# Ten VectorE pieces instead of twelve for a log series, with a new loop and end order

## The reference

```
xBC = zxbcdt[..., D_INNER:D_INNER + CONV_DIM]
dt = softplus(zxbcdt[..., -H_M:] + dt_bias)          # 8 heads
xBC = silu(conv_b + causal_conv4(xBC, conv_w))       # xh 512, B 128, C 128
A = -exp(A_log)
h_t = h_{t-1} * exp(dt_t * A) + (dt_t * xh_t) outer B_t
y_t = h_t @ C_t + D_skip * xh_t
out = resid + rms(y * silu(z), gnorm_w) @ out_proj_w
```

## Time and profile before

| what | value |
|---|---|
| median of three runs | 1319.52 us (1319.49 to 1320.14) |
| profiled execution: its span | 1319.5 us |
| granted TensorE clock | 1.00 in every window |
| TensorE matmuls busy | 1303.4 us, 99% |
| VectorE busy | 1193.6 us, 90%, 3032 instructions |
| ScalarE busy | 1131.2 us, 86% |
| GpSimd busy | 947.7 us, 72% |
| chain that ended last | TensorE 92%, VectorE 4%, GpSimd 2% |

### The profile page before, as it was taken

How to read it: one execution, slowest core, us unless ns; L and a number is a source line. 1 busy time by engine, 2 the same in 40 slices (tenths; PEclk the granted TensorE clock), 3 DMA queues, 4 the chain that set the end, 5 groups by cost and what they waited for, 6 DMA issues and landing times.

```text
span 1319.5 us, 43916 instructions
## 1 busy us (share of the span) xinstructions
PE 1303.4 (99%) x15877; PEld 1165.5 (88%) x15877; DVE 1193.6 (90%) x3032; ACT 1131.2 (86%) x3407; POOL 947.7 (72%) x1214
## 2 busy tenths in 40 slices
PE   8999999999999999999999999999999999999998
PEld 7888888999888898888998888899888889898887
DVE  6999999999999999999999999999999999999882
ACT  6778888898888898888898888899888899888866
POOL 4777777777777777777677777687777677677674
PEclk9999999999999999999999999999999999999999
DMA  6121122212122212122211122211122222011210
GB/s 208 48 74 50 50 74 78 78 49 67 50 70 78 78 50 66 50 70 78 78 57 59 50 70 78 78 60 57 50 70 78 77 82 62 17 51 58 66 49 25
DMA packets 41285, 87.03 MB, mean 66 GB/s; under 512 B 5744, under 2 KB 10992, under 8 KB 41072
## 3 DMA queue, kind: packets, MB, share of 16 engines
q1 hardware_dynamic: 40560, 83.93, 20.4%
q10 hardware_dynamic: 512, 0.31, 0.1%
HBM read 75.53 MB, written 8.68 MB: 64 GB/s over the span
## 4 chain that ended last, share of the span: by engine, by line
PE 92%; DVE 4%; POOL 2%; issue 1%; DMA 1%; ACT 1%; DVEq 0%; ACTq 0%; POOLq 0%
PE bank L332 28%; PE bank L442 11%; PE bank L573 7%; PE bank L432 5%; PE bank L399 5%; PE bank L456 5%; PE bank L556 5%; PE bank L587 4%; PE bank L692 4%; PE bank L627 3%; PE bank L380 3%; PE bank L648 3%; PE bank L677 2%; PE bank L490 2%; PE bank L436 1%; PE bank L531 1%
## 5 line engine op out<-in xcount | busy, mean ns | idle before, releaser
L991 DVE SCALAR_TENSOR_TENSOR ACC<-bank,cw,ACC 128x250 f32<-128x250 f32 (+2 forms) x576 | 264.5, 462 | 6.4 <-ACT ACC L1561 3.7
L332 PE MATMUL bank<-xnT,wnl 128*128 128x256 f32 x640 | 198.6, 310 | 1.7 <-DVE XC L1004 1.4
L1648 ACT ACTIVATE PC<-bank,stc 128x128 f32<-128x128 f32 x512 | 182.8, 388 | 8.0 <-DVE stc L1103 5.2
L332 PE MATMUL bank<-xnL,wnh 128*128 128x256 f32 x640 | 178.7, 279 | 0.0
L332 PE MATMUL bank<-xnT,wnh 128*128 128x256 f32 x640 | 178.3, 279 | 0.0
L835 DVE TENSOR_REDUCE sta<-bank 128x4 f32<-128x512 f32 x256 | 163.6, 672 | 2.8 <-PE bank L399 2.8
L1015 DVE TENSOR_TENSOR_SCAN L<-DB,id 128x1024 f32<-128x1024 f32 x64 | 146.6, 2290 | 2.2 <-DMA DB<-dec_scratch 2.2
L1967 POOL TENSOR_TENSOR PC<-PC,stc 128x512 f32<-128x512 f32 x128 | 132.4, 1043 | 11.7 <-DVE stc L1110 11.5
L1463 ACT ACTIVATE PTA<-bank 128x512 f32<-128x512 f32 x256 | 133.5, 629 | 6.8 <-PE bank L436 3.9
L332 PEld LDWEIGHTS bank<-xnT,wnl 128*128 128x128 f32 x640 | 120.4, 188 | 21.4 <-issue 16.2
L1922 POOL TENSOR_TENSOR XH<-XH,dtt 128x512 f32<-128x512 f32 x64 | 81.0, 1265 | 56.6 <-ACT XH L1578 56.6
(11 more groups left out here) (210 smaller groups left out, 4757.7 us busy)
## 6 DMA issues: line engine op xcount, KB each, us to landing
DB<-dec_scratch SPq DMA_DIRECT2D x64, 512.0 KB, 4.0
cT<-in_cT SPq DMA_DIRECT2D x64, 256.0 KB, 2.7
xt<-in_xt SPq DMA_DIRECT2D x32, 256.0 KB, 3.7
out_x<-X SPq DMA_DIRECT2D x32, 256.0 KB, 4.0
xT<-in_xT SPq DMA_DIRECT2D x31, 256.0 KB, 4.1
QM<-qm_rows SPq DMA_DIRECT2D x31, 128.0 KB, 4.0
XC<-in_win SPq DMA_DIRECT2D x2, 644.0 KB, 6.8
PTC<-in_wout SPq DMA_DIRECT2D x2, 256.0 KB, 4.6
```

The source lines that it names most:

```text
L332: mm = e.matmul(t[:, c0:c0 + T], wt[:, k, m:m + 128], x[:, k, :], start=(n == 0), stop=(n == 5))
L991: e.scalar_tensor_tensor(out=w, in0=t[:, 0:T].rearrange("p (b t) -> p b t", b=NB)[:, :, 0:125 + k], scalar=cw[:, c, k:k + 1], in1=w, op0=A ...
L1648: op = e.activation(PC[n % 4][:, p, :], t[:, p * 128:(p + 1) * 128], ACT.Exp, bias=stc[g % 4][:, 4 * i + p:4 * i + p + 1], accum_out=stc[g ...
```

## The change

The series is cut after fewer terms and its coefficients are fitted instead of 1, 1/3, 1/5 ... 1/13. `dc` has ten pieces: three Horner steps instead of five. In the loop and the end all engines have another order of blocks, and in `USES` some blocks another bank. In the fill the order of blocks is the one of before without the two pieces of each group. Two waits are new, both once in the run: `load_c(2)` waits for the mask rows' write, and `xs(0, 0)` for the small constants.

```diff
+ATANH = (1.000000004, 0.33333157341, 0.20012455137, 0.13980301434, 0.14089167199)
...
-            "dp": lambda g, i: (s_dc, 12 * g + 12), "bd": lambda g, i: (s_dk, g + 1),
+            "dp": lambda g, i: (s_dc, 10 * g + 10), "bd": lambda g, i: (s_dk, g + 1),
...
                     elif i == 3:
                         e.wait_ge(s_dq, g + 1)
-                        op = e.tensor_scalar(f, d[4], 1 / 13, None, ALU.mult)
-                    elif i < 9:
-                        op = e.scalar_tensor_tensor(out=f, in0=f, scalar=1 / (19 - 2 * i), in1=d[4], op0=ALU.add, op1=ALU.mult)
-                    elif i == 9:
-                        op = e.scalar_tensor_tensor(out=f, in0=f, scalar=1.0, in1=d[3], op0=ALU.add, op1=ALU.mult)
-                    elif i == 10:
+                        op = e.tensor_scalar(f, d[4], ATANH[4], None, ALU.mult)
+                    elif i < 7:
+                        op = e.scalar_tensor_tensor(out=f, in0=f, scalar=ATANH[7 - i], in1=d[4], op0=ALU.add, op1=ALU.mult)
+                    elif i == 7:
+                        op = e.scalar_tensor_tensor(out=f, in0=f, scalar=ATANH[0], in1=d[3], op0=ALU.add, op1=ALU.mult)
+                    elif i == 8:
...
             for g in range(NG - 9):
-                load_c(g + 6)
                 dec_out(g + 3)
                 dec_in(g + 3, 0)
-                load_m(g + 6)
+                load_c(g + 6)
+                load_u(g + 3)
                 load_x(g + 7)
-                load_u(g + 3)
                 dec_in(g + 3, 1)
                 load_t(g + 5)
                 store(g)
+                load_m(g + 6)
...
-                v(g + 7, 0)
                 bx(g + 4, 1)
+                v(g + 7, 0)
...
-                z(g + 5, 0)
                 v1(g + 3, 0)
+                z(g + 5, 0)
+                tn(g + 6, 0)
                 cp(g + 5, 2)
                 wp(g + 2, 0)
-                tn(g + 6, 0)
...
                 bd(g + 5, 0)
+                tn(g + 6, 1)
                 cp(g + 5, 5)
                 av(g + 6, 0)
                 av(g + 6, 1)
                 av(g + 6, 2)
                 av(g + 6, 3)
-                tn(g + 6, 1)
                 tC(g + 3, 0)
```

More of the change, by code:

```diff
@@ new lines, in vector @@
+            tap(2, 11); hs(1, 0); hs(1, 1); hg(1, 0); hg(1, 1); tap(2, 12); xc(2, 3); tap(2, 13); tap(2, 14); rc(3, 0)
+            tap(2, 15); xo(3, 0); tap(2, 16); tap(2, 17); bs(3, 0); bg(3, 0); xc(2, 4); xc(2, 5); sz(2, 1); xs(3, 0)
+            kk1(1, 0); rC(0, 3); hm(1, 0); hm(1, 1); scan(2, 0); mA(4, 0); rc(3, 1); mA(4, 1); xo(3, 1); kk1(1, 1)
+            mA(4, 2); mA(4, 3); bs(3, 1); bg(3, 1); lg(2, 0); xs(3, 1); x2(3, 0); x2(3, 1); yd(2, 0); mA(4, 4)
+            mA(4, 5); mA(4, 6); mA(4, 7); scan(2, 1); nl(3, 0); nl(3, 1); mC(1, 0); mC(1, 1); mC(1, 2); lg(2, 1)
@@ new lines, in vector @@
+            xc(3, 3); tap(3, 13); tap(3, 14); tap(3, 15); rc(4, 0); xo(4, 0); tap(3, 16); tap(3, 17); xc(3, 4)
+            bs(4, 0); xc(3, 5); bg(4, 0); hm(2, 0); hm(2, 1); sz(3, 1); kk1(2, 0); xs(4, 0); scan(3, 0); mA(5, 0)
+            kk1(2, 1); rC(1, 3); rc(4, 1); x2(4, 0); mA(5, 1); xo(4, 1); mA(5, 2); mA(5, 3); bs(4, 1); bg(4, 1)
+            lg(3, 0); xs(4, 1); x2(4, 1); mA(5, 4); mA(5, 5); nm(5, 0); yd(3, 0); mA(5, 6); mA(5, 7); scan(3, 1)
+            nl(4, 0); nl(4, 1); mC(2, 0); lg(3, 1); mC(2, 1); mC(2, 2); d0(4, 0); mC(2, 3); d0(4, 1); rC(2, 0)
@@ new lines, in vector @@
+            tap(4, 15); rc(5, 0); xo(5, 0); tap(4, 16); tap(4, 17); bs(5, 0); xc(4, 4); bg(5, 0); xc(4, 5); sz(4, 1)
+            hm(3, 0); hm(3, 1); kk1(3, 0); xs(5, 0); x2(5, 0); scan(4, 0); mA(6, 0); kk1(3, 1); rc(5, 1); xo(5, 1)
+            mA(6, 1); mA(6, 2); mA(6, 3); bs(5, 1); bg(5, 1); lg(4, 0); nm(6, 0); xs(5, 1); x2(5, 1); mA(6, 4)
+            mA(6, 5); yd(4, 0); mA(6, 6); mA(6, 7); nw(6, 0); scan(4, 1); nl(5, 0); nl(5, 1); mC(3, 0); lg(4, 1)
+            d0(5, 0); d0(5, 1); rC(3, 0); mC(3, 1); mC(3, 2); tap(5, 0); nm(6, 1)
@@ L1246, in vector @@
                 sz(g + 5, 0)
-                dc(g + 5, 8)
+                rC(g + 3, 2)
+                dc(g + 5, 9)
+                tap(g + 5, 7)
+                fin(g + 2, 0)
                 hs(g + 4, 0)
-                dc(g + 5, 9)
-                dc(g + 5, 10)
-                fin(g + 2, 0)
-                tap(g + 5, 6)
-                dc(g + 5, 11)
-                tap(g + 5, 7)
-                hg(g + 4, 0)
                 tap(g + 5, 8)
                 r1(g + 4, 1)
+                xc(g + 5, 2)
@@ L1374, in vector @@
-            hm(NG - 1, 1); rC(NG - 2, 3); kk1(NG - 1, 0); kk1(NG - 1, 1); mC(NG - 1, 0); mC(NG - 1, 1)
-            mC(NG - 1, 2); rC(NG - 1, 0); rC(NG - 1, 1); mC(NG - 1, 3); rC(NG - 1, 2); fin(NG - 2, 0); rC(NG - 1, 3)
-            fin(NG - 1, 0)
+                d0(g + 6, 1)
+            tap(NG - 4, 1); yd(NG - 5, 1); tap(NG - 4, 2); tap(NG - 4, 3); dc(NG - 4, 0); tap(NG - 4, 4)
+            r1(NG - 5, 0); nw(NG - 3, 1); tap(NG - 4, 5); dc(NG - 4, 1); dc(NG - 4, 2); hh(NG - 5, 0); rC(NG - 6, 1)
@@ new lines, in vector @@
+            fin(NG - 5, 0); tap(NG - 2, 7); r1(NG - 3, 1); tap(NG - 2, 8); hh(NG - 3, 1)
+            rC(NG - 4, 2); xc(NG - 2, 2); hm(NG - 3, 0); dk(NG - 2, 0); hs(NG - 3, 1); tap(NG - 2, 9); tap(NG - 2, 10)
+            tap(NG - 2, 11); tap(NG - 2, 12); hg(NG - 3, 1); tap(NG - 2, 13); tap(NG - 2, 14); tap(NG - 2, 15)
+            rc(NG - 1, 0); xo(NG - 1, 0); tap(NG - 2, 16); tap(NG - 2, 17); xc(NG - 2, 3); bs(NG - 1, 0)
+            rC(NG - 4, 3); xc(NG - 2, 4); hm(NG - 3, 1); xc(NG - 2, 5); bg(NG - 1, 0); xs(NG - 1, 0); scan(NG - 2, 0)
@@ new lines, in vector @@
+            tap(NG - 1, 15); hg(NG - 2, 1); tap(NG - 1, 16); hm(NG - 2, 0); xc(NG - 1, 4); tap(NG - 1, 17)
+            fin(NG - 4, 0); xc(NG - 1, 5); scan(NG - 1, 0); lg(NG - 1, 0); hm(NG - 2, 1); kk1(NG - 2, 0)
+            sz(NG - 1, 1); kk1(NG - 2, 1); yd(NG - 1, 0); scan(NG - 1, 1); lg(NG - 1, 1); mC(NG - 2, 0); rC(NG - 2, 0)
+            mC(NG - 2, 1); yd(NG - 1, 1); rC(NG - 2, 1); r1(NG - 1, 0); mC(NG - 2, 2); hh(NG - 1, 0); mC(NG - 2, 3)
+            fin(NG - 3, 0); hs(NG - 1, 0); r1(NG - 1, 1); hg(NG - 1, 0); rC(NG - 2, 2); hh(NG - 1, 1); hs(NG - 1, 1)
@@ L1378, in scalar @@
+            hg(NG - 1, 1); hm(NG - 1, 0); hm(NG - 1, 1); rC(NG - 2, 3); kk1(NG - 1, 0); kk1(NG - 1, 1); mC(NG - 1, 0)
+            mC(NG - 1, 1); mC(NG - 1, 2); rC(NG - 1, 0); mC(NG - 1, 3); rC(NG - 1, 1); fin(NG - 2, 0); rC(NG - 1, 2)
+            rC(NG - 1, 3); fin(NG - 1, 0)
         def scalar(e):
```

628 lines of the change are left out of this document (298 added, 330 removed), and 18 rows, old and new, of the table USES.

## The result

The changed kernel takes 1347.76 us (median of 4 runs, 1347.55 to 1348.07), the kernel before 1319.51 beside it: 2.1% slower, ratio 1.0208 (1.0195 to 1.0221). The profiled execution's span grew from 1319.5 to 1346.3 us. The forecast was 1315.0.

A forecast was written before the change was run, and what follows sets the result against it. TensorE was taken to bound the kernel (matmuls busy 1303.4 of 1319.5 us). Fill -0.2, loop -1.6, end gap -2.2 and last group -0.5 summed to -4.5, so 1315.0 us; range 1312.2 to 1318.6.

The forecast's parts named there:

- What bounds the kernel: Whole run: TensorE bounds it, so cutting VectorE work gains only where TensorE waits, 16.1 us outside its matmuls.
- Fill: Start of the run: group 0's taps 0.07 us earlier, later groups two instructions fewer; -0.2 us, between 0 and -0.9.
- Loop, the gain: Loop: moved `hm` ends `av`'s 0.11 us wait, 2.5 us in full; 0.07 an iteration taken, -1.6 us.
- Loop, the loss: Loop: no such term; only part of the gain returned through new neighbours, bound +1 us.
- the rivals: Other outcomes: gap stays 1317.2 (17%), loop gains nothing 1316.6 (15%), neither 1318.8 (7%), slower 1323.0 (9%).
- the slower case: Loop: `hm` ahead of the scan delays `lg` beyond 0.62 us of cover, so `y` starts late; 1323.0 us, 9%.
- the point of decision: Loop: slower from `lg` 0.75 us late on, where 23 x 0.13 = 3 us eats the other gains.
- End, the 2.2 us: Near 1240 us: TensorE's gap, read as instructions late behind SyncE's burst, goes with its new order; -2.2 us.
- End, the last group: From 1263 us: group 31's shorter series cuts TensorE's 0.64 us wait for `XC`; -0.5 us, between +0.5 and -1.5.
- The named edge: End: last `DB` behind stores of groups 27 and 28 lands by 1277.6, scan at 1278.16; holds by about half a microsecond.
- The signs: Expected in the profile: 39.4 us iterations, about 10 `PTA` waits, no gap near 1240, VectorE busy about 11 us less.
- The slower rival: Loop: `hm` making `lg` and `y` late, or late instructions behind SyncE's longer bursts; 1323.0 us, 9%.

The follow-up runs named there:

- e5: Changed kernel with the last three series pieces of VectorE's fill back in their old places: 1341.54 us, ratio 1.0163.
- e1: Changed kernel with ScalarE's loop copy `dd` put back ahead of `ac(·, 3)`: 1329.67 us, ratio 1.0082.
- e6: Changed kernel with the edits of e5 and e1, and the last piece also later in loop (behind `fin`) and end: 1320.30 us, ratio 1.0002.
- e8: Kernel before with only both `hm` of VectorE's loop moved behind `kk1`, ahead of `x2` and the scan: 1318.10 us, ratio 0.9983.
- e2: Changed kernel with `fin` moved ahead of the series' last piece in VectorE's loop: 1331.69 us, ratio 1.0100.
- e9: e6 with the old series of twelve pieces and old coefficients, so new orders without the cut: 1322.49 us, ratio 1.0018.
- e11: Kernel before, unchanged, run again for a second profile: 1318.73 us, profiled span 1316.9 us.
- e4: Kernel before with the ten-piece series, two middle Horner positions dropped, last three pieces left in place: 1319.67 us, ratio 1.0007.
- e3: Kernel before with the ten-piece series in the first ten of the twelve places, the last two dropped: 1358.09 us, ratio 1.0300.
- e7: Kernel before with SyncE's end alone changed: one store ahead of `dec_out(30)`, another behind the last `DB`: 1320.61 us, ratio 1.0008.
- e10: Kernel before with the edits of e4, e8 and e7 together: 1318.20 us, ratio 0.9989.
- e12: Kernel before with the edits of e4 and e8, SyncE's order as before: 1317.45 us, ratio 0.9991.

## Why the prediction was wrong, by its own steps

- **What bounds the kernel.** Right: TensorE, which is why a chain of other engines costs only when TensorE stands at its end. It was then read too narrowly. "So the price is worked out by place" is what failed: I worked out the places where TensorE waited before, and the change made new ones.
- **Fill.** For group 0 the chain was followed link by link and held: L974's wait (0.32 us measured), and the wait for `XC` at 0.43 us, expected near 0.4. "Later groups of the fill cover two instructions fewer with a TensorE that doesn't wait for them" is the sentence that failed. I took the moved last piece for two instructions fewer in groups 1 to 5 also, and never asked there when ScalarE's copy comes. There `dd` stands behind blocks that wait for TensorE, and L974 waited 0.9 to 1.9 us. The term was -0.2 us and measured +10.4 ahead of group 7. About 4 of them are the fill's last pieces (e5) and about 1 the late copy of ScalarE's loop, which begins with group 4 (e1, e6). Some 2.4 are the late `DB` and the clock behind it, which nothing in the prediction covers and no run explains. The other 2.8 stay with the last piece late everywhere (e6); most of them come where the engines go over to the new loop order.
- **Loop, the gain.** Right in kind and about in size: e8 gives 39.39 us an iteration by moving `hm` alone, 0.11 us, the whole of the excess in the earlier trace rows, where I had taken 0.07. The new order as a whole works 39.30 to 39.32 (e1, e2, e6, e9), and the further 0.08 us of TensorE's own time is left open: its neighbours and its banks changed together, and I made no run that parts them.
- **Loop, the loss.** Missing from the sum and from the rivals. This is the step that failed most: the loop's term was -1.6 us, and it measured +11.7 over 21 iterations, 0.55 in each, because nothing in the prediction followed the last piece and `fin` behind it to `sT`. The order of `dd` and `ac(·, 3)`, of `dc(·, 9)` and `fin`, was there to be read, and the row with the price was there as well: L970 waited about 0.4 us for `dtt` in 23 groups, and `fin` was ahead of the last of the twelve pieces. The slacks that I took for `sT` were those of the old VectorE order. I weighed `hm` and `lg` as the slower case, with a wait on another engine of 0.13 us as the point of decision; the wait that came was 0.67.
- **End, the 2.2 us.** Wrong, though the gap near 1240 and the scan's wait for `DB` are indeed gone from the changed kernel. The gap is an event of single executions (e11, also e4 and e8 have none with the same burst), and a term of a sum must not rest on one. In e11, without it, the span is 1316.9. The scan's wait, 2.18 us in the earlier trace rows, isn't fixed either: it is 1.30 in e4 and none in e11. That the rule on packet-wise turns between queues in **DMA: Bandwidth & Descriptors** of the Trainium skill (queues, rings and completion order) spoke against a full queue as the cause stays as it was: in e11 the burst drains with three q8 packets in the stretch and no gap, which agrees with it; one execution with the gap and two packets doesn't decide it.
- **End, the last group.** Forecast -0.5, measured +3.5 for groups 28 to 30 and +3.3 after them against e11 (+1.1 against the execution with the gap). e6, with the last piece late everywhere, takes 2.9 and 1.9 off. The named edge, the last `DB` behind two stores, did not decide: the stores of groups 27 and 28 were issued from 1295.40 on, `DB` at 1299.04, and the scan at 1304.37 had no wait for it; the only wait of a scan for `DB` in the run, 0.9 us, is at 72.4.
- **The signs.** The 5 waits for `PTA` (about 10 forecast) and the missing gap came as forecast beside a loss of 28 us, so they told nothing of the total. The iteration (40.05, not 39.4) and VectorE's busy time (7.9 us more, not 11 less) did.
- **The slower rival.** It was given 9% and 1323, a loss of 3.5 us; the mechanism was another and the loss eight times that (28.2). That the sign was among the rivals is no merit of the reasoning. The range reached to 1318.6 on that side, where one link that had not been followed is worth 0.5 us in each of 23 iterations.

## What to carry to other kernels

Removing instructions from an engine that runs in order moves everything behind them, and the piece that waits for another engine moves with them. Price the position of the waiting instruction ahead of the work saved: find what it waits for, when that comes, and what stands behind it on its own engine and who needs that. Two versions with the same ten pieces differ by 38 us through the places of the last three (e3, e4), while the two pieces that were cut were worth nothing measurable in one order (e4) and about 2 us in the other (e9).

When an order is planned for n pieces and run with fewer, drop them where nothing waits, and keep the ones with semaphores of other engines at their old places. And before a one-time gap becomes a term of a sum, look at a second execution.

## What the runs showed of the hardware

- A gap of 2.2 us on TensorE without a releaser came in one execution of the kernel before and in none of the other thirteen profiled executions. The profiled spans of that one program are 1319.5 and 1316.9 us.
- A small instruction of VectorE can be held until an instruction of GpSimd ends: `hm` on 128x1 takes 0.15 us alone and up to 0.72 beside a TENSOR_TENSOR of GpSimd, and then ends 0.01 to 0.02 us behind it (46 of 46). Not every pair does this: two `hm` lie inside a 128x1 TENSOR_TENSOR of GpSimd and take 0.13 and 0.15 us.
- Behind a pause of 1.49 us in the fill TensorE's granted clock was 0.79 over the next 8 us (changed kernel); behind one of 0.45 us at the same place it stayed at 1.00 (e1).
- Stores issued within 0.1 us behind a 512 KB load went with a wait of the scan for that load of 1.79 and 1.69 us (e7, e10), against 0.20 and 0.16 (e11, e8). That they cause it isn't shown: the loads took 6.8 and 6.7 us to land with them, and 5.4, 5.1 and 6.6 without (e11, e8, e12).
